# TensorE finds a batch's live chunks with eight nested bodies in place of four loops of two (perceiver block, one core)

## The chip, the cores and the metric

The kernel runs on one core of a Trainium2 chip. The metric is the device time of one execution in microseconds (us), the median of several runs. The kernel is written in Bass: every engine (TensorE or PE, VectorE or DVE, ScalarE or ACT, GpSimd or POOL, SyncE or SP) has a program of its own, and they meet only through semaphores.

## The reference

A block of three layers on x (8 batches, 128 rows, 512 wide): cross-attention to a context, self-attention, and a gated MLP with ternary weights. Only the first matters here:

```python
def xattn(x, context, mask, W_q, W_k, W_v, W_o, b_o):      # x (8,128,512), context (8,2048,384), mask (8,2048)
    q = (x @ W_q).reshape(b, n, 8, 64)
    k = (context @ W_k).reshape(b, j, 8, 64)
    v = (context @ W_v).reshape(b, j, 8, 64)
    sim = einsum('bihd,bjhd->bhij', q, k) / 8
    sim = where(mask[:, None, None, :], sim, max_neg)
    out = einsum('bhij,bjhd->bihd', softmax(sim), v).reshape(b, n, 512)
    return out @ W_o + b_o
x = x + xattn(layernorm(x), ctx, mask, ...)
x = x + self_attention(layernorm(x), ...)
x = x + ffn(layernorm(x), ...)
```

The mask is true only for the last keys of a batch, from 0 to 512 of the 2048, a number drawn for each batch. Keys that are masked out of a batch with any live key have no weight in the softmax.

## The kernel before, in words

The context of a batch is cut into NC = 8 chunks of 256 keys. A chunk with no live key needn't be computed. So the kernel first makes 64 bits, one for each chunk of each batch (a batch without any live key counts all its chunks as live), and each engine loads them into two registers (`live_chunks`, L239). All engines then walk the same list: a loop over the 8 batches (L773 on PE), in it a loop over four groups of two chunks (L778), and in that `live_in_window` (L268). It takes the group's two bits into `left`, shifts the word, and runs its body as often as bits are set: a branch (`If_ne(left, 0)`, L274), two register operations that clear the lowest bit (L275, L276), the body, and in it once more the branch and the body. A group without a live chunk thus jumps over two bodies. At the end of a batch `next_batch` moves the words on by eight bits (L256 to L258).

The body (`chunk`, L677 on PE, L1064 on ScalarE, L1463 on VectorE) does the attention of the current chunk, interleaved with the work for the next live one: `turn_context` (L647, L651) transposes the next chunk's context, `keys` and `values` project it in split precision (three products each, L587). `scores` (L690) for head pairs 0 to 3, `turn` (L705), which transposes the probabilities, and `attend` (L717) are the current chunk's. VectorE's `top` (L1472) takes a head's scores with the mask's bias, writes them to `probs` and the running maximum to `negm`; scores of the next pair wait for it. ScalarE exponentiates (L1069) and then casts the context's high part (L1052). The context of a chunk (cx) is loaded by SyncE.

Behind a batch's last chunk PE does `project_output` of the batch before (L764, from batch 1 on), `turn_output` (L745: the normalised output on_c, which VectorE makes at L1517) and from batch 2 on `turn_norm` (L753). ScalarE and VectorE split the transposed results into high and low parts (onT_hi, onT_lo), VectorE also makes the low part of the next batch's queries (qT_lo). Then each engine walks to the next batch's first live chunk on its own; nothing but the body's semaphores holds one engine to another.

Of the kernel before, what the change touches and what calls it, by code (L numbers as in the profile page):

```python
# [5 lines left out]
ALU = mybir.AluOpType  # L6
# [19 lines left out]
def bass_perceiver_block_kernel(nc, x, ctx_768, mask, xa_wq, xa_wk, xa_wv, xa_wo, xa_bo,  # L26
# [17 lines left out]
    NC = S // CHUNK  # L44
# [11 lines left out]
    with ExitStack() as ctx:  # L56
# [182 lines left out]
        def live_chunks(eng):  # L239

            eng.wait_ge(code_packed, START + 1)
            words = []
            for w in range(CODES // 2):
                low_half = eng.value_load(code[0:1, 2 * w:2 * w + 1], min_val=0, max_val=65535)
                high_half = eng.value_load(code[0:1, 2 * w + 1:2 * w + 2], min_val=0, max_val=65535)
                bits = eng.alloc_register(f"live_chunks{w}")
                eng.reg_mov(bits, high_half)
                eng.reg_alu(bits, bits, 16, ALU.logical_shift_left)
                eng.reg_alu(bits, bits, low_half, ALU.bitwise_or)
                words.append(bits)  # L250
            return words, eng.alloc_register("live_flag")

        def next_batch(eng, words, carry):

            low_word, high_word = words
            eng.reg_alu(carry, high_word, 32 - NC, ALU.logical_shift_left)  # L256
            eng.reg_alu(high_word, high_word, NC, ALU.logical_shift_right)
            eng.reg_alu(low_word, low_word, carry, ALU.bitwise_or)  # L258
# [6 lines left out]

        WINDOW = 2

        def live_in_window(eng, words, left, flag, body):  # L268

            eng.reg_alu(left, words[0], (1 << WINDOW) - 1, ALU.bitwise_and)  # L270
            eng.reg_alu(words[0], words[0], WINDOW, ALU.logical_shift_right)

            def nest(depth):
                with eng.If_ne(left, 0):  # L274
                    eng.reg_alu(flag, left, 1, ALU.subtract)  # L275
                    eng.reg_alu(left, left, flag, ALU.bitwise_and)  # L276
                    body()
                    if depth > 1:
                        nest(depth - 1)

            nest(WINDOW)

        UNITS = 2 * PAIRS

# [289 lines left out]
        def _(pe):  # L574
# [42 lines left out]
            words, flag = live_chunks(pe)  # L617
            left = pe.alloc_register("window_left")
# [122 lines left out]
            def turn_output(b):  # L741

                pe.wait_ge(on_done, START + b + 1)
                for k in range(DK):
                    last = tr(bank[5][:, k * P:(k + 1) * P], on_c[:, k * P:(k + 1) * P], ident[:])  # L745
                last.then_inc(onT_ps, 1)

            def turn_norm(b):

                pe.wait_ge(xn_c_done, START + b + 1)  # L750
                pe.wait_ge(lnT_lo, START + b)
                for k in range(DK):
                    last = tr(bank[6][:, k * P:(k + 1) * P], xn_c[:, k * P:(k + 1) * P], ident[:])  # L753
                last.then_inc(lnT_ps, 1)

            def project_output(b):

                pe.wait_ge(xo_done, START + b)
                n = 0

                for a, c in (("hi", "hi"), ("hi", "lo"), ("lo", "hi")):
                    pe.wait_ge(onT_lo if a == "lo" else onT_hi, START + b + 1)
                    for k in range(DK):
                        last = mm(bank[4][:], part(onT, a)[:, k, :], part(wo, c)[:, k, :], start=(n == 0), stop=(n == 3 * DK - 1))  # L764
                        n += 1
                last.then_inc(xo_ps, 1)
# [6 lines left out]
            with pe.Fori(0, B) as b:  # L773
                def live_chunk():
                    chunk(b, pe.snap(done))
                    pe.reg_add(done, done, 1)

                with pe.Fori(0, NC // WINDOW) as c:  # L778
                    live_in_window(pe, words, left, flag, live_chunk)
                next_batch(pe, words, flag)  # L780
                chunks = pe.snap(done)
                pe.wait_ge(negm_done, START + H * chunks)
                with pe.If(b > 0):
                    project_output(b - 1)
                turn_output(b)
                with pe.If(b > 1):
                    turn_norm(b - 2)
# [222 lines left out]
        def _(act):  # L1010
# [113 lines left out]
            with act.Fori(0, B) as b:  # L1124
                def live_chunk():
                    chunk(b, act.snap(done))
                    act.reg_add(done, done, 1)

                with act.Fori(0, NC // WINDOW) as c:
                    live_in_window(act, words, left, flag, live_chunk)  # L1130
                next_batch(act, words, flag)
                with act.If(b < B - 1):
                    query_high(b + 1, act.snap(done))
                with act.If(b > 0):
                    projected(b - 1)
                output_high(b)
                with act.If(b > 1):
                    norm_high(b - 2)
# [209 lines left out]
        def _(dve):  # L1348
# [207 lines left out]
            with dve.Fori(0, B) as b:  # L1556
                def live_chunk():
                    chunk(b, dve.snap(done))
                    dve.reg_add(done, done, 1)

                with dve.Fori(0, NC // WINDOW) as c:
                    live_in_window(dve, words, left, flag, live_chunk)
                next_batch(dve, words, flag)
                chunks = dve.snap(done)
                with dve.If(b > 1):
                    norm_stats(b - 2)
                normalise(b, chunks)
                with dve.If(b > 1):
                    norm(b - 2)
                with dve.If(b < B - 1):  # L1570
                    query_low(b + 1)
                output_low(b)
                with dve.If(b > 1):
                    norm_low(b - 2)
# [274 lines left out]
```

## Time and profile before

| what | value |
|---|---|
| median of 3 runs | 767.38 us (766.2 to 770.09) |
| profiled execution, its own time | 768.35 us |
| its span, first to last instruction | 765.2 us |
| TensorE's granted clock, mean | 0.945 |
| PE matmul busy | 666.9 us (87% of the span) |
| VectorE busy | 443.9 us (58%) |
| ScalarE busy | 356.4 us (47%) |
| PE in the chain that ended last | 66% |

The span is divided by stage: projections of the queries to about 57 us, the attention over the context with its walk to about 377 us, then the self-attention and the MLP. Rows with PEldq, DVEq or ACTq are the engines' sequencers: branches and register operations, which count as busy for no engine. The instruction queues q8 and q14 in the DMA part bring code.

### The profile page before, as it was taken

The numbers are of one execution on the slowest core, as the hardware profiler recorded it, in microseconds if no ns is written. First come the engines' busy times: TensorE is split into PE (matmuls) and PEld (weight loads), VectorE is DVE, ScalarE is ACT, GpSimd is POOL, SyncE is SP. The second block draws the span as 40 slices with busy tenths as digits, with TensorE's granted clock in tenths as the row PEclk, the third lists the DMA queues.
The fourth block names the chain that finished last, engine by engine and source line by source line (L and its number), as shares of the span: only waits on it lengthen the run. The fifth ranks groups of instructions, "written<-read, shape, count | busy, mean of one in ns | idle before, by whom it ended". The sixth has DMA issues, their size and how long they took to land.

```text
span 765.2 us, 14274 instructions
## 1 busy us (share of the span) xinstructions
PE 666.9 (87%) x4217; PEld 524.4 (69%) x4244; DVE 443.9 (58%) x960; ACT 356.4 (47%) x846; POOL 109.0 (14%) x143
## 2 busy tenths in 40 slices
PE   2898698979889779979879889999999899889996
PEld 1677587868778668868758667777777778534553
DVE  6823444554545453545567756666666544699974
ACT  2234233434434333434410146666666443568984
POOL 2681000010100110010100012222221100012121
PEclk9999798979989897989989989999999999999999
DMA  8000000000000000004169834445553343000111
GB/s 314 26 23 24 24 2 21 22 22 22 2 21 22 22 2 21 22 22 140 69 205 301 290 110 166 166 166 165 166 165 139 136 140 124 1 1 15 27 27 41
DMA packets 40067, 64.91 MB, mean 85 GB/s; under 512 B 4056, under 2 KB 20440, under 8 KB 40032
## 3 DMA queue, kind: packets, MB, share of 16 engines
q1 hardware_dynamic: 40032, 64.45, 25.1%
q8 instruction: 21, 0.34, 0.2%
q14 instruction: 14, 0.11, 0.0%
HBM read 53.95 MB, written 10.49 MB: 84 GB/s over the span
## 4 chain that ended last, share of the span: by engine, by line
PE 66%; DVE 13%; issue 9%; DMA 4%; ACT 3%; DVEq 3%; POOL 1%; SPq 1%; ACTq 0%; POOLq 0%
PE bank L587 35%; PE bank L717 6%; PE bank L949 5%; PE bank L705 3%; DMA absw<-in_L_ffn_w_down_dram 3%; PE bank L690 3%; PE bank L957 2%; PE bank L864 2%; DVE asum L1607 2%; DVE tern L1657 2%; PE bank L606 2%; DVE xn_a L1374 1%; PE bank L841 1%; PE bank L899 1%; PE bank L852 1%
## 5 line engine op out<-in xcount | busy, mean ns | idle before, releaser
L1069 ACT ACTIVATE probs<-probs,negm 128x256 f32<-128x256 f32 x104 | 52.1, 501 | 87.1 <-DVE negm L1472 86.5
L1472 DVE CUSTOM_DVE_ANT_0 probs<-bank,bias,negm_old 128x256 f32<-128x256 f32 x104 | 46.0, 480 | 42.4 <-PE bank L690 42.4
L949 PE MATMUL bank<-w_T,xqT 128*128 128x512 bf16 x248 | 57.3, 379 | 5.3 <-ACT xqT L1252 2.0
L717 PEld LDWEIGHTS bank<-v_sb,pT 128*128 128x128 f32 x416 | 52.3, 191 | 5.5
L484 POOL TENSOR_TENSOR rstd<-var_eps,neg_half 128x1 f32 (+1 forms) x16 | 10.0, 625 | 320.9 <-DVE var_eps L1535 249.8
L1363 DVE TENSOR_TENSOR kT_lo<-bank,kT_hi 128x512 fp32r<-128x512 f32 x28 | 19.4, 692 | 62.0 <-ACT kT_hi L1058 62.0
L717 PE MATMUL bank<-v_sb,pT 128*128 128x64 f32 x416 | 54.7, 274 | 0.0
L1062 ACT COPY v_sb<-bank 128x512 f32<-128x512 f32 x28 | 15.1, 590 | 76.5 <-PE bank L717 73.5
L690 PE MATMUL bank<-kT_hi,qT_hi 64*128 64x256 f32 x104 | 23.0, 433 | 29.6 <-issue 27.2
L949 PEld LDWEIGHTS bank<-w_T,xqT 128*128 128x128 bf16 x256 | 24.1, 98 | 34.9 <-issue 2.9
L587 PE MATMUL bank<-cxT_hi,wk_hi 128*128 128x256 f32 x168 | 38.4, 342 | 4.6 <-ACT cxT_hi L1052 4.6
L690 PEld LDWEIGHTS bank<-kT_hi,qT_hi 64*128 64x128 f32 x104 | 11.9, 212 | 39.0 <-issue 28.7
L530 POOL TENSOR_TENSOR p_even<-p_even,rsum 128x512 f32<-128x512 f32 x16 | 18.1, 1131 | 118.6 <-DVE rsum L1636 118.6
L705 PE MATMUL bank<-ident,probs 128*128 128x128 f32 x208 | 33.9, 289 | 0.0
L1607 DVE TENSOR_REDUCE asum<-absw 128x3072 f32 x8 | 26.8, 3351 | 10.6 <-DMA absw<-in_L_ffn_w_down_dram 10.6
L587 PEld LDWEIGHTS bank<-cxT_hi,wk_hi 128*128 128x128 f32 x168 | 27.3, 217 | 8.2 <-ACT cxT_hi L1052 7.4
L1626 DVE COPY kT<-bank 128x512 f32<-128x512 f32 x16 | 11.1, 692 | 37.0 <-PE bank L587 37.0
L587 PE MATMUL bank<-cxT_lo,wk_hi 128*128 128x256 f32 x168 | 31.8, 301 | 0.5 <-DVE cxT_lo L1363 0.5
L587 PE MATMUL bank<-cxT_hi,wk_lo 128*128 128x256 f32 x168 | 32.2, 305 | 0.0
L1173 ACT ACTIVATE p_odd<-bank,nmax 128x128 f32<-128x128 f32 x64 | 22.7, 371 | 15.7 <-DVE nmax L1632 15.7
L1187 ACT ACTIVATE tern_raw<-tern_raw,wscale 128x1024 f32<-128x1024 f32 x24 | 26.9, 1163 | 4.0 <-DVE tern_raw L1651 4.0
L587 PEld LDWEIGHTS bank<-cxT_lo,wk_hi 128*128 128x128 f32 x168 | 27.0, 209 | 0.8 <-DVE cxT_lo L1363 0.7
(236 smaller groups left out, 1692.1 us busy)
## 6 DMA issues: line engine op xcount, KB each, us to landing
tern_dram<-tern SPq DMA_DIRECT2D x8, 768.0 KB, 5.4
tstage<-tern_dram SPq DMA_DIRECT2D x8, 768.0 KB, 4.4
cx<-in_ctx_dram SPq DMA_DIRECT2D x14, 384.0 KB, 3.0
absw<-in_L_ffn_w_gate_dram SPq DMA_DIRECT2D x8, 512.0 KB, 3.8
absw<-in_L_ffn_w_up_dram SPq DMA_DIRECT2D x8, 512.0 KB, 5.4
absw<-in_L_ffn_w_down_dram SPq DMA_DIRECT2D x8, 512.0 KB, 6.8
tern_raw<-in_L_ffn_w_gate_dram SPq DMA_DIRECT2D x8, 512.0 KB, 6.4
tern_raw<-in_L_ffn_w_up_dram SPq DMA_DIRECT2D x8, 512.0 KB, 7.1
```

What stands on the lines that cost most here:

```text
L530: nc.gpsimd.tensor_tensor(p, p, r, ALU.mult).then_inc(pn_done, 1)
L587: last = mm(to, left(k, a), right(k, b), start=(n == 0), stop=(n == 3 * nk - 1))
L690: last = mm(bank[3 + j][:, 0:CHUNK], part(qT, a)[o:o + DH, g, :], part(kT, c)[o:o + DH, g, :], start=(a == c), stop=(a == "lo"))
L705: last = tr(bank[5 + g % 2][:, at:at + P], probs[:, 2 * g + j, t * P:(t + 1) * P], ident[:])
L717: last = mm(bank[7][:, h * DH:(h + 1) * DH], pT[:, g % 2, at:at + P], v_sb[:, t, h * DH:(h + 1) * DH], start=(t == 0), stop=(t == CT - 1))
L949: last = mm(bank[3 + 2 * which + c % 2][:], xqT[:, u, k * P:(k + 1) * P], w_T[:, which, k, c * 512:c * 512 + 512], start=(k == 0), stop=(k ...
L1069: fn(probs[:, h, :], probs[:, h, :], ACT.Exp, bias=negm[:, h:h + 1], scale=-1.0, accum_out=csum[:, h:h + 1]).then_inc(p_done, 1)
L1173: last = fn(p2[u % 2][j][:, g * P:(g + 1) * P], bank[2 + j][:, g * P:(g + 1) * P], ACT.Exp, bias=nmax2[:, j, g:g + 1], scale=SCALE, accum_ ...
L1187: made = fn(piece, piece, ACT.Copy, bias=ROUND, scale=wscale[:, w:w + 1])
L1363: return tt(to, of, f32(hi), ALU.subtract)
L1472: nc.vector.tensor_tensor_reduce(probs[:, h, :], bank[3 + h % 2][:, 0:CHUNK], bias[:], -SCALE, negm_old[:, h:h + 1], ALU.add, ALU.min, neg ...
L1607: red(asum[:, bass.ds(g, 1), :].rearrange("p a w -> p (a w)"), absw[u][:], AX_X, ALU.add, apply_absolute_value=True).then_inc(absw_done, 1)
```

## The change

`live_in_window` gets its number of bits as an argument. PE calls it once for a batch with all NC = 8 bits, so that its code has eight nested bodies, and has no loop over groups any more. ScalarE and VectorE keep their loops of four groups of two. SyncE has its own walk, chunk by chunk, and keeps it.

```diff
-        def live_in_window(eng, words, left, flag, body):
-
-            eng.reg_alu(left, words[0], (1 << WINDOW) - 1, ALU.bitwise_and)
-            eng.reg_alu(words[0], words[0], WINDOW, ALU.logical_shift_right)
+        def live_in_window(eng, words, left, flag, body, size=WINDOW):
+
+            eng.reg_alu(left, words[0], (1 << size) - 1, ALU.bitwise_and)
+            eng.reg_alu(words[0], words[0], size, ALU.logical_shift_right)
...
-            nest(WINDOW)
+            nest(size)
...
-                with pe.Fori(0, NC // WINDOW) as c:
-                    live_in_window(pe, words, left, flag, live_chunk)
+                live_in_window(pe, words, left, flag, live_chunk, NC)
                 next_batch(pe, words, flag)
```

PE's program at the start of the batch loop, before. L773 is the loop over batches, L778 the loop over groups, L270 to L276 the walk, L690 the first scores of body 0:

```order
L773 UNCONDITIONAL_BRANCH
L778 UNCONDITIONAL_BRANCH
L270 REGISTER_ALU
L271 REGISTER_ALU
L274 COMPARE_AND_BRANCH
L275 REGISTER_ALU
L276 REGISTER_ALU
```

and the same place after the change:

```order
L773 UNCONDITIONAL_BRANCH
L270 REGISTER_ALU
L271 REGISTER_ALU
L274 COMPARE_AND_BRANCH
L275 REGISTER_ALU
L276 REGISTER_ALU
```

The walk enters body 0 directly. The end of the last body and the batch's tail on PE, before (L717 is the last `attend`, L764 `project_output`):

```order
L717 MATMUL bank<-v_sb,pT 128x64 x4
L776 REGISTER_ALU
L274 UNCONDITIONAL_BRANCH
L778 REGISTER_ALU
L778 COMPARE_AND_BRANCH
L256 ISA
L258 REGISTER_ALU
```

and after, at the end of body 7 (the lines below the change are one lower):

```order
L717 MATMUL bank<-v_sb,pT 128x64 x4
L776 REGISTER_ALU
L274 UNCONDITIONAL_BRANCH
L256 ISA
L258 REGISTER_ALU
```

The loop's back edge over groups is gone. Between the two places PE's program had two bodies and now has eight; the matmuls of its whole program go from 2114 to 2810 as they are written (a body has 116). The programs of the other engines are the same instruction by instruction.

## Rows read from the trace of the kernel before

**Rows 1.** The page, section 2: TensorE's granted clock in 40 slices, tenths.
```profile
PEclk9999798979989897989989989999999999999999
```

**Rows 2.** PE sequencer: xcount, ns min/median/max, first to last start in us.
```profile
L776 PEldq ALU_OP  x13: 32/32/32, 80.6 to 371.3; - x13
...
L778 PEldq COMPARE_BRANCH  x32: 67/208/242, 61.0 to 371.5; - x32
...
L274 PEldq COMPARE_BRANCH  x4: 75/210/215, 86.2 to 88.8; - x4
```

**Rows 3.** Timeline, starts of batches 1 and 3: start, us, work [idle before <-releaser].
```profile
85.14 1.11 PE L745 MATMUL bank<-ident,on_c 128*128 128x128 f32 x4 [2.42 <-DVE on_c L1517]
...
89.56 0.58 PE L690 MATMUL bank<-kT_hi,qT_hi 64*128 64x256 f32 x2 [3.31 <-issue]
...
90.15 0.42 PE L690 MATMUL bank<-kT_hi,qT_lo 64*128 64x256 f32 x2
...
92.22 0.58 PE L690 MATMUL bank<-kT_hi,qT_hi 64*128 64x256 f32 x2 [0.18 <-DVE negm L1472]
...
160.04 0.66 PE L745 MATMUL bank<-ident,on_c 128*128 128x128 f32 x4 [0.66 <-DVE on_c L1517]
```

**Rows 4.** Chain in order of time: start, us, what; starts of batches 1, 3.
```profile
88.17 0.06 DVEq L274
...
90.58 0.05 DVEq L274
...
91.27 0.11 DVE probs L1472
...
165.71 0.05 DVEq L274
...
166.38 0.11 DVE probs L1472
```

**Rows 5.** Batch 0's start: timeline, then the branch L274 on PE and on VectorE.
```profile
63.98 0.58 PE L690 MATMUL bank<-kT_hi,qT_hi 64*128 64x256 f32 x2 [2.99 <-issue]
...
65.16 0.48 DVE L1472 CUSTOM_DVE_ANT_0 probs<-bank,bias,negm_old 128x256 f32<-128x256 f32 x1 [6.92 <-PE bank L690]
...
L274 PEldq COMPARE_BRANCH  x1: 3535/3535/3535, 57.3 to 57.3; - x1
...
L274 DVEq COMPARE_BRANCH  x1: 50/50/50, 62.7 to 62.7; - x1
```

**Rows 6.** DMA queues: packets, MB, share; 36-94, 100-380 (q1 is all), 400-702 us.
```profile
q8 instruction: 6, 0.10, 0.8%
...
q1 hardware_dynamic: 4502, 8.14, 9.0%
...
q8 instruction: 15, 0.25, 0.3%
```

**Rows 7.** Stretches: length, busy us (xcount) by engine, PEclk, DMA share, GB/s.
```profile
138.30:156.50 18.20, 17.33 (x133) 15.46 (x134) 9.20 (x29) 8.41 (x25) 0.00 (x0) 1.00 0.08 23
89.55:110.80 21.25, 20.89 (x133) 18.70 (x134) 8.51 (x28) 7.45 (x23) 0.00 (x0) 0.80 0.06 19
400.00:702.00 302.00, 277.37 (x1777) 209.30 (x1795) 198.62 (x340) 157.72 (x399) 42.40 (x53) 0.98 0.42 143
84.40:98.10 13.70, 9.30 (x44) 7.99 (x44) 4.75 (x14) 4.10 (x12) 0.00 (x0) 0.50 0.09 29
```

**Rows 8.** Ends of batches 0, 1: branches of PE, then timeline of 1.
```profile
L274 PEldq COMPARE_BRANCH  x1: 429/429/429, 80.7 to 80.7; - x1
...
L274 PEldq COMPARE_BRANCH  x1: 207/207/207, 108.8 to 108.8; - x1
...
L783 PEldq COMPARE_BRANCH  x1: 82/82/82, 109.7 to 109.7; - x1
...
110.61 1.18 PE L764 MATMUL bank<-wo_hi,onT_hi 128*128 128x512 f32 x4
...
113.46 0.60 PE L745 MATMUL bank<-ident,on_c 128*128 128x128 f32 x4
```

## The prediction

> **What bounds the kernel now.** I read the page first: in the first half of the span, where the attention over the context runs, PEclk goes between 7 and 9 tenths [rows 1], so the clock falls there again and again. The change touches only how PE finds its live chunks, so the question is who is late at a batch's start and at its end. The chunk body runs 13 times (L776 x13) [rows 2] in 8 batches: so three batches have one live chunk and five two, always the last ones of the batch's eight, so PE, VectorE and ScalarE each pass three empty groups of two before the one that works. For PE that is 4 groups x 8 batches, the 32 of L778 [rows 2].
>
> The price of an empty group is in the register rows of PE's sequencer [rows 2]: two ALU operations, a taken COMPARE_BRANCH of 207 ns at L274, an ALU and another taken branch of 208 ns at L778; four L274 branches lie between 86.2 and 88.8 us, so a group costs PE (88.8 - 86.2) / 3 = 0.87 us, three of them 2.6 us. The timeline of batch 1's start shows this as PE idle for 3.31 us "<-issue" [rows 3]. That looks like 8 x 2.6 = 21 us to gain. But the chain of work over the same stretch [rows 4] doesn't run through PE there: it runs through VectorE's own walk (four branches DVEq L274, the first at 88.17 and the last at 90.58, so 0.80 us a group) to the first row maximum at 91.27. PE's first scores are out at 90.15 + 0.42 = 90.57, or 0.7 us before VectorE can read them. What PE does after the transposes waits for VectorE again (scores 1 at 92.22, "<-DVE negm" [rows 3]). The chain passes through the same DVEq rows at the start of batch 3: the last branch at 165.71, the maximum at 166.38 [rows 4]. So at seven of the eight starts VectorE, whose walk is not changed, ends last.
>
> **The change part by part.**
> Three empty groups leave PE at each start. Batches 1 to 7: PE's scores 0 and its transposes of the context come up to 2.6 us earlier, and then PE waits for the same negm at the same time. Gain 0: VectorE's walk covers it. If that cover were gone too, the 3.31 us of idle PE would be worth at most 2.6 us a batch, 18 us.
> Batch 0 is different. VectorE's last L274 branch is at 62.7 [rows 5], and in batch 1 it needs 91.27 - 90.58 = 0.7 us from there to the first maximum [rows 4], so it is ready at 63.4; it starts at 65.16, released by PE [rows 5], whose scores begin at 63.98 after 2.99 us of issue. Now they can begin where the queue of values ends, at 61.0, and be out at 62.0. VectorE then bounds: the gain is 65.16 - 63.4 = **1.8 us**, once (ends: 0, if something else is late, and 2.99, PE's whole gap).
> The first scores and the transposes also let cx be loaded earlier; its consumer is a whole chunk of 18 us away [rows 7], so 0. SP, POOL, VectorE and ScalarE have the same instructions as before.
>
> Seven copies of code come in. At the end of a batch's last live chunk the branch at L274 now jumps over six or seven bodies, not over one or none. What a jump to code that isn't loaded costs PE is in the trace once: the first L274 branch of the kernel, over two bodies that have not been run, took 3535 ns at 57.3 us, against 207 for the others [rows 5]. It cost nothing there, since PE still had matmuls queued to 61.0. Six packets of PE's instruction queue (q8, 16 KB each) came in between 36 and 94 us, and none from 100 to 380 us, where q1 is the only queue listed [rows 6], while the loop ran seven more times. So PE keeps the whole loop of before. How much is that? Between 400 and 702 us 15 packets came while PE ran 1777 matmuls and 1795 weight loads [rows 6, 7]: about 240 of these to a packet, some 255 with register work. One body is 266 matmuls and loads (133 and 134 in 18.2 us) [rows 7] and some 25 others, so 1.15 packets; the loop of before is two bodies and the batch's tail, 2.6 packets; that of after is eight and a tail, **9.5 packets** from top to end. Of these only the top, bodies 0 and 1 and the tail are ever run, about 3 or 4 packets with the next one fetched ahead each time, 6 or 7. The trace shows that 2.6 packets in a row stay; it does not show whether two pieces 7 packets apart do.
>
> The Trainium skill (Runtime: NRT & Kernel Launch, Instruction fetch mechanics) says that an engine holds its current window of two pages and that a taken branch out of it stalls for a fetch; the loop of before is 2.6 packets long and fetched nothing in seven passes, so for PE the trace does not agree with the two pages. The same section gives TensorE room for 2048 instructions, that is 8 pages; by that capacity the loop of before fits and the one of after, 9.5 packets, does not.
>
> Price of one such miss at a batch's end. The branch takes 3.53 instead of 0.21 us, 3.3 more. In batch 1 it is issued at 108.80, the next one (L783) at 109.7, so project_output could be issued at about 110.1; it begins at 110.61, without a gap behind the chunk [rows 8]. With 3.3 us more it begins at 113.4, 2.8 us late, and since turn_output follows it at once (113.46, no idle) all of that is lost. In batches 2 to 7 the sequencer is as far ahead, but turn_output waits anyway: in batch 3, PE is idle for 0.66 us before 160.04 [rows 3], which leaves 2.0 to 2.1. VectorE has work of its own queued there, which may cover a part; between nothing and 2.0 I take 1.7, near the upper end, since the whole start of the next batch hangs on what turn_output gives. In batch 0 there is no projection; the miss from 80.7 [rows 8] runs to 84.3, the register work of 1.2 us after it (L274 to the first matmul, as in batch 1) to 85.5, and turn_output stands at 85.14 behind on_c [rows 3], so 0.3 is left. One miss is certain, in batch 0, where that code is first reached: **+0.3 us**.
>
> Sum for the profiled execution, 768.35 us: -1.8 + 0.3 = 766.9. The median of the three runs is 767.38, 1.0 lower, so **766.0 us** if the code stays loaded. Below 0.5% (3.8 us) a measurement of this kernel can't tell from no change.
>
> **The rivals.**
> Recurring fetch (slower). Where the code at the tail and that at the top push each other out, the branch at the end of each batch costs 3.3 us again: 0.3 + 2.8 + 6 x 1.7 = 13.3, less 1.8: +11.5, so 779 us. If only batches with two live chunks do it (they fetch one packet further), 0.3 + 5 x 1.7 - 1.8: +7, 774 us. For it: 9.5 packets, more than any loop of the trace; and six packets came between 36 and 94 us although the loop's code is only 2.6 long, so some may have come twice. Against: none came for the next seven passes. This decides from a loss of 3.8 us on, that is from three batches with a miss. The back edge can miss too; PE has 2.6 + 0.7 = 3.3 us of slack there, just the price, so this alone costs nothing. Chance 0.32. The Trainium skill's 2048 instructions, in the section named above, speak for this rival.
> Two misses a batch (slower). If body 0 also has to be fetched again in its middle, PE stalls with full queues behind it: 1.3 to 3.3 us in seven batches, +9 to +23 on top, 788 to 802 us. For: a straight run into the next packet has always been fetched ahead in the trace, so against it more than for. Chance 0.06.
> Clock (faster). PE is granted 0.50 of its clock (1.2 GHz) from 84.4 to 98.1 us, behind the idle stretch of batch 1's start, and 1.00 (2.4 GHz) from 138.3 to 156.5 [rows 7]; a first chunk takes 21.25 us (batch 1, clock 0.80), a second one 18.2 at 1.00. Scores that come 2.6 us earlier split the idle stretch in another way. If that kept the clock up in three of eight starts, 3 x 2.5 = 7.5 us, plus the 1.8: 758 us. Against: PE's busy time is the same and the gap of 3.3 us is only moved behind the transposes, which could as well take 2 to 3 us. Chance 0.10 for the faster side.
> That the change doesn't do what it says gets nothing: the order of the instructions shows PE's bodies eight deep and the loop of groups gone.
>
> **How the numbers follow.** Code stays loaded, 766.0: 0.52 (764 to 769 with the ends of batch 0's gain and one more miss). Recurring fetch 0.32 and two misses 0.06, 0.38 slower by over 0.5%. Faster by over 0.5%: 0.10. The range takes in the forecast less 3.5 us of the clock's case, and the recurring fetch with its bound of 2.0 us a batch (0.3 + 2.8 + 6 x 2.0 - 1.8 = +13.3, 781) and 2 us for the clock: **762.5 to 783**. Left out are two misses and most of the faster case, 0.14.
>
> **What would show it.** Right: L1472's first maximum of batch 0 near 63.4 us; PE's gap before the scores of batches 1 to 7 down from 3.3 to about 0.7 us, with a new one of about 3 us "<-DVE negm" behind the transposes; chain through DVEq L274 as before; L274 branches of PE at 207 ns but for one of 3.5 us near 79 us; q8 packets silent from 100 to 380 us. Wrong: L274 branches of 3.5 us in most batches with q8 packets beside them (recurring fetch); stalls inside a chunk (two misses); fewer stretches at 0.50 (clock); or batches 1 to 7 each shorter by more than 1 us, which would mean that VectorE is not the last at their start.

## The result and the profile after

The changed kernel takes 775.15 us (median of 6 runs, 771.14 to 780.39) against 766.79 us for the kernel before (6 runs): ratio 1.011, 95% interval 1.0076 to 1.0144. It is slower by 8.4 us. The profiled execution of the changed kernel took 775.04 us with a span of 772.9 us, 7.7 us more than that of before. Lines of the changed kernel are one lower behind L778 (VectorE's maximum is L1471, ScalarE's exponential L1068, the branch at the tail L782).

The page of the changed kernel, its sections 1 to 4, where [rows 1, 6] have their like:

```profile
PE 668.5 (86%) x4244; PEld 523.8 (68%) x4244; DVE 443.4 (57%) x960; ACT 356.6 (46%) x846; POOL 108.9 (14%) x143
...
PEclk9999798988989987998979999999999999999999
...
q8 instruction: 25, 0.41, 0.2%
...
PE 69%; issue 10%; DVE 10%; POOL 4%; ACT 3%; DVEq 3%; ACTq 0%; POOLq 0%
```

and the code queue's line of the kernel before:

```profile
q8 instruction: 21, 0.34, 0.2%
```

PE does the same work. The code queue q8 brought 25 packets against 21. I compared the two traces by VectorE's first maximum of each batch (L1472, L1471 in the changed kernel), in us:

| | before | changed | later by |
|---|---|---|---|
| batch 0 | 65.16 | 63.41 | -1.75 |
| batch 1 | 91.27 | 93.65 | +2.38 |
| batch 2 | 118.89 | 120.70 | +1.81 |
| batch 3 | 166.38 | 173.66 | +7.28 |
| batch 4 | 213.99 | 221.54 | +7.55 |
| batch 5 | 260.09 | 269.34 | +9.25 |
| batch 6 | 289.97 | 300.13 | +10.16 |
| batch 7 | 337.24 | 347.89 | +10.65 |
| batch 7, second chunk | 355.84 | 368.32 | +12.48 |

Four things happened: a gain at batch 0, a step of 4.1 us at its end, one of 5.5 us at the end of batch 2, and a drift of 5.2 us from batch 3 to the end. Behind the attention 4.8 of the 12.5 us came back.

**Batch 0's start** went as forecast. Timeline of the changed kernel, against [rows 5]:

```profile
60.90 0.38 PE L690 MATMUL bank<-kT_hi,qT_hi 64*128 64x256 f32 x2
...
63.41 0.48 DVE L1471 CUSTOM_DVE_ANT_0 probs<-bank,bias,negm_old 128x256 f32<-128x256 f32 x1 [5.19 <-issue]
```

PE's scores begin at 60.90 right behind the queue of values, and VectorE, ready at 63.4, is now the last.

**The two steps** are long branches. The branches of PE's sequencer in the changed kernel (xcount, ns min/median/max, first to last start), by stretch: about 80 us, 84 us, 156 us, and all from 165 to 390 us:

```profile
L274 PEldq COMPARE_BRANCH  x1: 3872/3872/3872, 80.2 to 80.2; - x1
...
L782 PEldq COMPARE_BRANCH  x1: 2892/2892/2892, 84.5 to 84.5; - x1
...
L274 PEldq COMPARE_BRANCH  x1: 3854/3854/3854, 156.1 to 156.1; - x1
...
L274 PEldq COMPARE_BRANCH  x13: 66/66/208, 191.4 to 383.9; - x13
```

and what PE waited for behind them, timeline:

```profile
87.52 1.11 PE L745 MATMUL bank<-ident,on_c 128*128 128x128 f32 x4 [5.36 <-issue]
...
160.69 0.79 PE L764 MATMUL bank<-wo_hi,onT_hi 128*128 128x512 f32 x1 [2.64 <-issue]
163.15 1.44 PE L764 MATMUL bank<-wo_hi,onT_hi 128*128 128x512 f32 x3 [1.67 <-issue]
164.39 1.91 PE L764 MATMUL bank<-wo_lo,onT_hi 128*128 128x512 f32 x4
166.09 1.72 PE L764 MATMUL bank<-wo_hi,onT_lo 128*128 128x512 f32 x4
167.65 0.60 PE L745 MATMUL bank<-ident,on_c 128*128 128x128 f32 x4
```

At the end of batch 0 the jump over seven bodies took 3.87 us; the tail's code lies across two packets, and the next branch in it (L782) took 2.89 us, because the second packet wasn't there either. turn_output came at 87.52 in place of 85.14 us [rows 3]. At the end of batch 2, the first batch with two live chunks, there is one more of 3.85 us, and inside project_output a second wait of 1.67 us. PE's clock also fell to half at about 160.5 us, after the idle stretch, so that most of the twelve matmuls of project_output, which are 512 wide, ran at 1.2 GHz (length, busy us of PE, PEld, DVE, ACT, POOL with xcount, PEclk, DMA share, GB/s):

```profile
160.40:167.30 6.90, 4.94 (x11) 3.77 (x12) 2.00 (x5) 0.00 (x0) 0.56 (x1) 0.52 0.01 2
```

No branch was long after that: the longest of the other 13 took 208 ns.

The code queue shows the order at batch 2. One packet came between 150 and 156 us, that is before the long branch at 156.1, while PE was still in the second chunk; two more came between 156 and 166 us; from 166 to 380 us there was none:

```profile
q8 instruction: 1, 0.02, 1.0%
...
q8 instruction: 2, 0.03, 1.6%
```

**The drift** has no fetch in it. It comes in batches 3 (+0.3), 4 (+1.7), 5 (+0.9), 6 (+0.5) and 7 (+1.8), inside the first chunk. The first chunks of the changed kernel all take about the same (20.4 to 20.5 us in batches 3, 4, 6 and 7); those of the kernel before took 20.2, 18.8, 19.9 and 18.6 us, so most of the drift is that two short ones are gone. Maxima of batch 4's two chunks, changed kernel:

```profile
221.54 0.48 DVE L1471 CUSTOM_DVE_ANT_0 probs<-bank,bias,negm_old 128x256 f32<-128x256 f32 x1 [2.87 <-issue]
...
241.99 0.48 DVE L1471 CUSTOM_DVE_ANT_0 probs<-bank,bias,negm_old 128x256 f32<-128x256 f32 x1
```

and before:

```profile
213.99 0.48 DVE L1472 CUSTOM_DVE_ANT_0 probs<-bank,bias,negm_old 128x256 f32<-128x256 f32 x1 [2.87 <-PE bank L690]
...
232.75 0.48 DVE L1472 CUSTOM_DVE_ANT_0 probs<-bank,bias,negm_old 128x256 f32<-128x256 f32 x1
```

20.45 us in place of 18.76. The stretches at half clock there (columns as above), of the changed kernel:

```profile
221.90:228.70 6.80, 6.04 (x30) 5.52 (x30) 2.36 (x10) 3.51 (x11) 0.00 (x0) 0.51 0.01 5
```

and of the kernel before:

```profile
210.70:217.50 6.80, 4.79 (x24) 4.08 (x25) 2.70 (x10) 1.83 (x6) 0.00 (x0) 0.50 0.17 46
```

Both are 6.8 us at 0.50 (1.2 GHz). Before, it began with PE idle ahead of the scores, 3.3 us ahead of the maximum, and PE had 4.8 us of work in it. In the changed kernel it began 0.4 us behind the maximum and PE had 6.0 us of work in it, which at 2.4 GHz takes about half as long (four matmuls 512 wide: 1.91 us here, 1.08 there, in the rows of L587 below). By that the changed kernel loses 3.0 us there and the other 2.4, so 0.6 of the 1.7 us is told by the amount of work in the stretch. The rest would be in which work it was (ahead of the maximum, or behind it); I didn't separate that. The kernels below that drift too have 20.3 to 20.4 us in this chunk with another stretch, 10.2 us long from about 3 us ahead of the maximum, so neither the length of the stretch nor the work in it gives the time by itself. stall_like, batch 4:

```profile
218.00:228.20 10.20, 8.16 (x40) 7.25 (x40) 3.24 (x11) 3.51 (x11) 0.00 (x0) 0.50 0.12 39
```

**What came back.** Behind the attention PE waits for the mean of the MLP's weights. Before:

```profile
439.98 0.59 PE L815 MATMUL bank<-asum,ones 128*128 128x3 f32 x2 [2.57 <-DVE asum L1614]
440.43 2.05 PE L587 MATMUL bank<-ln_T_hi,wqk_even_hi 128*128 128x512 f32 x4
442.28 1.91 PE L587 MATMUL bank<-ln_T_hi,wqk_even_lo 128*128 128x512 f32 x4
443.99 1.91 PE L587 MATMUL bank<-ln_T_lo,wqk_even_hi 128*128 128x512 f32 x4
```

and changed:

```profile
450.26 0.39 PE L814 MATMUL bank<-asum,ones 128*128 128x3 f32 x2
450.51 1.17 PE L587 MATMUL bank<-ln_T_hi,wqk_even_hi 128*128 128x512 f32 x4
451.52 1.08 PE L587 MATMUL bank<-ln_T_hi,wqk_even_lo 128*128 128x512 f32 x4
452.44 1.08 PE L587 MATMUL bank<-ln_T_lo,wqk_even_hi 128*128 128x512 f32 x4
```

Before, PE had been waiting 2.57 us there and its clock had fallen, so the next twelve matmuls took until 445.9; in the changed kernel the weights were in time, nothing was idle and they took 3.0 us. That is 2.5 us of the 4.8; the mean itself is only 10.3 us later instead of 12.5.

### The profile page after: what moved, and what is told of

Read it like the earlier page. It is cut to its first block, busy times and chain, and to the rows that moved or that the text cites. A ratio compares the mean times of both kernels' runs of the same rounds, so it can differ in the third digit from the quotient of the medians.

```text
span 772.9 us, 14167 instructions
## 1 busy us (share of the span) xinstructions
PE 668.5 (86%) x4244; PEld 523.8 (68%) x4244; DVE 443.4 (57%) x960; ACT 356.6 (46%) x846; POOL 108.9 (14%) x143
## 4 chain that ended last, share of the span: by engine, by line
PE 69%; issue 10%; DVE 10%; POOL 4%; ACT 3%; DVEq 3%; ACTq 0%; POOLq 0%
PE bank L587 39%; PE bank L717 6%; PE bank L948 5%; PE bank L705 3%; PE bank L690 2%; PE bank L956 2%; PE bank L863 2%; DVE tern L1656 2%; POOL x_all L513 1%; PE bank L840 1%; PE bank L898 1%; PE bank L764 1%; PE bank L851 1%; ACT cxT_hi L1051 1%; DVE h_f L1761 1%
## 5 line engine op out<-in xcount | busy, mean ns | idle before, releaser
L1068 ACT ACTIVATE probs<-probs,negm 128x256 f32<-128x256 f32 x104 | 52.1, 501 | 85.7 <-DVE negm L1471 85.1
L1471 DVE CUSTOM_DVE_ANT_0 probs<-bank,bias,negm_old 128x256 f32<-128x256 f32 x104 | 46.0, 480 | 40.9 <-issue 27.2
L717 PEld LDWEIGHTS bank<-v_sb,pT 128*128 128x128 f32 x416 | 52.3, 191 | 5.5
L717 PE MATMUL bank<-v_sb,pT 128*128 128x64 f32 x416 | 54.7, 274 | 0.0
L690 PE MATMUL bank<-kT_hi,qT_hi 64*128 64x256 f32 x104 | 22.0, 420 | 33.8 <-DVE negm L1471 28.7
L587 PE MATMUL bank<-cxT_hi,wk_hi 128*128 128x256 f32 x168 | 39.7, 352 | 5.2 <-ACT cxT_hi L1051 5.2
L690 PEld LDWEIGHTS bank<-kT_hi,qT_hi 64*128 64x128 f32 x104 | 10.9, 205 | 43.6 <-DVE negm L1471 32.1
L587 PEld LDWEIGHTS bank<-cxT_hi,wk_hi 128*128 128x128 f32 x168 | 28.5, 226 | 8.7 <-ACT cxT_hi L1051 8.0
L587 PE MATMUL bank<-cxT_lo,wk_hi 128*128 128x256 f32 x168 | 33.9, 316 | 0.5 <-DVE cxT_lo L1362 0.5
L587 PE MATMUL bank<-cxT_hi,wk_lo 128*128 128x256 f32 x168 | 33.3, 313 | 0.0
L587 PEld LDWEIGHTS bank<-cxT_lo,wk_hi 128*128 128x128 f32 x168 | 28.7, 223 | 0.8 <-DVE cxT_lo L1362 0.7
L587 PEld LDWEIGHTS bank<-cxT_hi,wk_lo 128*128 128x128 f32 x168 | 28.4, 223 | 0.0
```

The source lines that it names most:

```text
L587: last = mm(to, left(k, a), right(k, b), start=(n == 0), stop=(n == 3 * nk - 1))
L690: last = mm(bank[3 + j][:, 0:CHUNK], part(qT, a)[o:o + DH, g, :], part(kT, c)[o:o + DH, g, :], start=(a == c), stop=(a == "lo"))
L717: last = mm(bank[7][:, h * DH:(h + 1) * DH], pT[:, g % 2, at:at + P], v_sb[:, t, h * DH:(h + 1) * DH], start=(t == 0), stop=(t == CT - 1))
L1068: fn(probs[:, h, :], probs[:, h, :], ACT.Exp, bias=negm[:, h:h + 1], scale=-1.0, accum_out=csum[:, h:h + 1]).then_inc(p_done, 1)
L1471: nc.vector.tensor_tensor_reduce(probs[:, h, :], bank[3 + h % 2][:, 0:CHUNK], bias[:], -SCALE, negm_old[:, h:h + 1], ALU.add, ALU.min, neg ...
```

## The experiments

Ratios are to the kernel before, timed beside each run on the same chip: its medians there were 764.46 us (pe_four, pe8_late, skip_all, pe8_skip), 763.82 us (stall_like, skip_dve_act, pe_one, dve_late) and 764.56 us (pe8_both, skip_again).

**pe_four: half as much code.** PE walks two groups of four bodies.

```diff
-                live_in_window(pe, words, left, flag, live_chunk, NC)
+                with pe.Fori(0, NC // 4) as c:
+                    live_in_window(pe, words, left, flag, live_chunk, 4)
```

> PE walks two groups of four nested bodies; the loop is about 4.9 packets of code from top to end, so it would fit where 2.6 does. Theory A (neighbour): PE's instruction buffer fetches the next packet ahead without regard to what is already in it, and that pushes out the tail, which was fetched out of order; misses come once each time a longer straight run is made for the first time: L274 branches of 3.5 us or more at 57 us (hidden), at the end of batch 0 and at the end of batch 2, the first with two live chunks, then none. Attention end 3 to 10 us later than before (377 us), time 768 to 773 us. Rival B (capacity): the misses of the eight-body kernel come because 9.5 packets do not fit; then there is only the hidden one at 57 us here, and the time is 765 to 768 us.

Measured: 769.94 us, ratio 1.006 (1.0035 to 1.0085). PE's branches L274 at 58.8, 80.5 and 153.9 us, and all later ones:

```profile
L274 PEldq COMPARE_BRANCH  x1: 3508/3508/3508, 58.8 to 58.8; - x1
...
L274 PEldq COMPARE_BRANCH  x1: 3402/3402/3402, 80.5 to 80.5; - x1
...
L274 PEldq COMPARE_BRANCH  x1: 3672/3672/3672, 153.9 to 153.9; - x1
...
L274 PEldq COMPARE_BRANCH  x17: 75/207/213, 186.5 to 378.6; - x17
```

Three long branches, at the three places that theory A names, and none at the ends of the five batches that follow, though the loop's code is half as long. So the misses don't come from 9.5 packets being too many; rival B falls. The maxima are 0.7 us early at batch 2, 2.6 us late at batch 3, and 7.2 us late at the end: a drift of 4.6 us here too.

At batch 0's end this kernel has the single miss that the prediction had priced: the tail's next branch (L783 here) is short in all batches, and turn_output stands at 85.00 us behind on_c, as before the change (85.14 [rows 3]). The single miss cost nothing that can be seen.

```profile
L783 PEldq COMPARE_BRANCH  x8: 77/77/249, 84.6 to 379.5; - x8
...
85.00 0.65 PE L745 MATMUL bank<-ident,on_c 128*128 128x128 f32 x4 [2.48 <-DVE on_c L1517]
```

**pe8_both: the longest straight run first.** The changed kernel, in which every batch has two live chunks: in three batches one chunk is computed whose keys are all masked, so its time has 3 chunks more and isn't compared.

```diff
+                eng.reg_alu(bits, bits, 0x40404040, ALU.bitwise_or)
```

> The changed kernel with the bit of chunk 6 set in every batch on every engine: the three batches with one live chunk now compute one more, whose keys are all masked, so 3 chunks of 18 us are added and only the branches are to be compared. Theory A (a straight run that gets farther than any before it fetches the next packet over the tail's): batch 0 already runs bodies 0 and 1, so the farthest run is made before the tail is first fetched; long branches only at the end of batch 0 (one or two), none at the end of batch 1, 2 or later. Rival I (the tail's packets fall out of the buffer for another reason, with time or after some passes): one more at the end of batch 2 or nearby.

Measured: 821.53 us in one run. Branches of PE (L275 is the walk's here, L783 the tail's), at 98 us, at 102 us, and all of the walk from 110 us on:

```profile
L275 PEldq COMPARE_BRANCH  x1: 3822/3822/3822, 98.1 to 98.1; - x1
...
L783 PEldq COMPARE_BRANCH  x1: 3177/3177/3177, 102.4 to 102.4; - x1
...
L275 PEldq COMPARE_BRANCH  x20: 66/70/217, 129.4 to 431.1; - x20
```

Two long branches at batch 0's end, where the tail is first reached, and none at batch 2 or elsewhere. Rival I falls. Together with pe_four and the packet that came ahead of the long branch of batch 2: the tail's packet is lost when the straight run gets one packet farther than before for the first time, as if the packet fetched ahead took its place. That it takes that place is an inference from these orders, not a thing that a row shows, and pe8_both is one run.

**stall_like: the stalls without the code.** The kernel before with empty loops on PE where the long branches were.

```diff
                 with pe.Fori(0, NC // WINDOW) as c:
                     live_in_window(pe, words, left, flag, live_chunk)
+                with pe.If(b < 3):
+                    with pe.If(b < 1):
+                        with pe.Fori(0, 17) as idle:
+                            pass
+                    with pe.If(b > 1):
+                        with pe.Fori(0, 10) as idle:
+                            pass
```

> The kernel before, with its two bodies, and empty loops on PE in the places of the changed kernel's long branches: 17 passes (some 6.2 us; the two branches there took 3.7 + 2.8 us too long) behind batch 0's chunk, 10 passes (3.6 us) behind batch 2's, two short branches in the others. Theory A2 (three late fetches are the whole loss): the maxima move as in the changed kernel, by +4 us at batch 1, +7 to +8 at batch 3 and the rest, up to +12, in batches 4 to 7 without any stall there; time 772 to 777 us. Rival G (the eight bodies cost something else too, in every batch): +4 and +4 only, nothing in batches 4 to 7, time 768 to 771 us.

Measured: 777.17 us, ratio 1.016 (1.0095 to 1.0226). The maxima are later by 3.76 (batch 1), 3.84 (2), 7.50 (3), 7.40 (4), 8.91 (5), 9.71 (6), 10.13 (7) and 11.89 us at the last chunk. With two bodies of code and no packet of q8 from 94 us to the end of the attention, the whole pattern is there, the drift too (4.4 us). So stalls at those two places are enough for the loss, and rival G falls: nothing is left that the eight bodies would have to cost in a batch where their code is loaded. The match is not exact: the loops idle PE 1 us longer at batch 0, batch 0's gain is mostly missing, and the loss by the medians is 13.3 us, more than the changed kernel's 8.4, with intervals that overlap. The timeline of batch 0's end:

```profile
88.90 1.11 PE L745 MATMUL bank<-ident,on_c 128*128 128x128 f32 x4 [6.41 <-issue]
```

**pe8_late: PE's scores at their old time.** The changed kernel with seven empty passes (2.6 us) ahead of PE's walk.

```diff
+                with pe.Fori(0, 7) as idle:
+                    pass
                 live_in_window(pe, words, left, flag, live_chunk, NC)
```

> The changed kernel with a loop of seven empty passes ahead of PE's walk at every start of a batch, so that PE's first scores come at the old time again (2.6 us later). Theory C (clock): in the changed kernel part of the loss, some 5 of the 12.5 us by the end of the attention, comes in batches 3 to 7 without any fetch, because the earlier scores move the stretch at 0.50 from the idle time into the dense part of the chunk; then the first chunks of batches 4 and 7 (22.8 us maximum to maximum in the changed kernel's trace, against 18.8 before) lose less and the time falls to 769 to 773 us. Rival D (the loss is all in the three misses): the time stays at 775 or rises by the 1.8 us of batch 0.

Measured: 776.24 us, ratio 1.0143 (1.008 to 1.0206). The maxima are +9.37 at batch 4, +11.01 at batch 5 and +14.19 at the last chunk: the drift from batch 3 on is 5.0 us, as in the changed kernel. Theory C falls in its form: the earlier scores don't cause the drift. What the kernels with a drift share (the changed one, pe_four, stall_like, pe8_late) is that everything from batch 3 on is 2.6 to 9.2 us later, and that the first chunks of batches 4 and 7 take 20.3 to 20.5 us with PE's half-clock stretch elsewhere: in the changed kernel 6.8 us long from 0.4 us behind the maximum, in the other three 10.2 us long from about 3 us ahead of it. What decides between these wasn't tried, and the cause of the drift stays open. Read the other way, the run says that PE's 2.6 us at a start are free when the code is there: only batch 0's gain (1.6 us at its maximum) is lost.

**skip_all and skip_again: the walk of all three engines.** Two new operations and a branch ahead of the groups; the last two chunks have code of their own.

```diff
+        def skip_dead(eng, words, rest, left, flag, body):
+
+            eng.reg_alu(rest, words[0], (1 << (NC - WINDOW)) - 1, ALU.bitwise_and)
+            eng.reg_alu(words[0], words[0], NC - WINDOW, ALU.logical_shift_right)
+            with eng.If_ne(rest, 0):
+                with eng.Fori(0, NC // WINDOW - 1) as c:
+                    live_in_window(eng, [rest], left, flag, body)
+            live_in_window(eng, words, left, flag, body)
...
-                with pe.Fori(0, NC // WINDOW) as c:
-                    live_in_window(pe, words, left, flag, live_chunk)
+                skip_dead(pe, words, rest, left, flag, live_chunk)
```

and the same for ScalarE and VectorE.

> All three engines test the first six bits of a batch with one branch and jump over a loop of three groups where none is set; the last two chunks have code of their own (four bodies on each engine). Theory E (VectorE ends last at a batch's start): its walk loses 2.4 us and gains about 0.4, so each of batches 1 to 7 begins 2.0 us earlier and batch 0 1.8 us: 14 to 16 us less, 751 to 754 us, plus up to 3 us for a miss or two. Rival F (something else, ScalarE or the loads, stands right behind VectorE): less than 8 us gained, 760 or more.

> The kernel of skip_all once more, for its interval: 745 to 749 us, ratio to before 0.970 to 0.980.

Measured: 746.8 us, ratio 0.9727 (0.9652 to 0.9803); again, with more executions, 742.99 us, ratio 0.9726 (0.9696 to 0.9756). It beats both kernels, by 21 us that of before. Batch 1's start in the second of them (L700 is the scores', L1482 the maximum's line):

```profile
84.61 0.58 PE L700 MATMUL bank<-kT_hi,qT_hi 64*128 64x256 f32 x2 [1.04 <-issue]
...
86.29 0.48 DVE L1482 CUSTOM_DVE_ANT_0 probs<-bank,bias,negm_old 128x256 f32<-128x256 f32 x1 [1.29 <-PE bank L700]
```

The maximum is 5.0 us earlier than the 91.27 of [rows 4], 2.5 of it from batch 0, 2.5 at this start. More was gained than the 14 to 16 us that were expected of the walk. The attention of this kernel (columns as above):

```profile
57.00:355.00 298.00, 270.87 (x1865) 235.61 (x1864) 149.24 (x454) 125.73 (x353) 16.37 (x19) 0.94 0.09 30
```

against that of the kernel before:

```profile
57.00:377.00 320.00, 278.51 (x1867) 242.61 (x1866) 152.28 (x456) 126.26 (x354) 16.17 (x21) 0.90 0.09 28
```

PE has 7.6 us less of busy time for the same matmuls, at a mean clock of 0.94 in place of 0.90. So a part of the gain is clock; how much of it wasn't separated, and that the shorter idle stretches are what keeps it up is likely but not shown.

**pe8_skip: the change with that skip on the others.** ScalarE and VectorE as in skip_all, PE as in the changed kernel.

> PE as in the changed kernel (eight nested bodies), ScalarE and VectorE with the one-branch skip. By theory E the changed kernel's 775 us fall by 2.0 us for each of seven starts, to 759 to 763 us, still behind skip_all by the misses (7 to 10 us). By rival F 768 us or more.

Measured: 754.01 us, ratio 0.9853 (0.9803 to 0.9903). By the ratios that is 1.3% or 10 us behind skip_all, by the medians 7 us, and the three long branches are there (3.8, 2.7 and 3.4 us). It is better than expected by 5 us; I didn't look for the cause.

**skip_dve_act: PE alone keeps the slow walk.**

> ScalarE and VectorE with the one-branch skip, PE with its four groups as before. Theory E (VectorE ends last at a start, PE 0.7 us ahead of it): once VectorE is 2 us earlier PE's walk is the last, so only 0.7 us a start is left, some 5 us of the 17.7 that the skip on all engines gained: 758 to 761 us. Rival H (PE's walk never matters): the whole 17 us, 747 us.

Measured: 757.87 us, ratio 0.9917 (0.9889 to 0.9945). Batch 1's start (L699 is the scores'):

```profile
89.19 0.58 PE L699 MATMUL bank<-kT_hi,qT_hi 64*128 64x256 f32 x2 [3.40 <-issue]
...
90.36 0.48 DVE L1482 CUSTOM_DVE_ANT_0 probs<-bank,bias,negm_old 128x256 f32<-128x256 f32 x1 [3.15 <-PE bank L699]
```

VectorE now waits for PE's scores. The gain is 6 of the 18 us by which skip_all's median is lower, near the 5 that 0.7 us a start would give; rival H falls.

**pe_one: a longer walk on PE.** One body, eight groups; the edit is against the changed kernel.

```diff
-                live_in_window(pe, words, left, flag, live_chunk, NC)
+                with pe.Fori(0, NC) as c:
+                    live_in_window(pe, words, left, flag, live_chunk, 1)
```

> PE walks eight groups of one body: six or seven empty ones before the first live chunk in place of three, so 3.0 to 3.5 more at 0.87 us each. With 0.7 us of slack at a start PE becomes the last by 2 to 2.5 us a start: +16 to +20 us, and 0 to 0.5 us between two live chunks; 780 to 786 us. If PE's walk had far more slack than 0.7 us: under 772. No long branch except perhaps the first, since the code is 1.5 packets.

Measured: 783.2 us, ratio 1.0251 (1.0205 to 1.0298), +19 us. Batch 1's start:

```profile
98.16 0.73 PE L690 MATMUL bank<-kT_hi,qT_hi 64*128 64x256 f32 x2 [6.61 <-issue]
...
99.32 0.48 DVE L1472 CUSTOM_DVE_ANT_0 probs<-bank,bias,negm_old 128x256 f32<-128x256 f32 x1 [6.07 <-PE bank L690]
```

PE idles 6.61 us, and VectorE waits 6.07 us for it.

**dve_late: a longer walk on VectorE.** The kernel before with three empty passes ahead of VectorE's. They were taken for 1.1 us; the trace shows 0.8.

```diff
+                with dve.Fori(0, 3) as idle:
+                    pass
                 with dve.Fori(0, NC // WINDOW) as c:
```

> The kernel before with a loop of three empty passes (1.1 us) ahead of VectorE's walk. By theory E each of batches 1 to 7 starts 1.1 us later, batch 0 not at all (VectorE waits 1.8 us for PE there): +7 to +8 us, 771 to 773 us. If VectorE's walk is not last: +0 to 2 us.

Measured: 770.88 us, ratio 1.0083 (1.0055 to 1.0111), +6.4 us by the ratio. At batch 1 the maximum is at 91.89 and PE's scores were out at 90.43:

```profile
89.42 0.58 PE L690 MATMUL bank<-kT_hi,qT_hi 64*128 64x256 f32 x2 [3.32 <-issue]
...
90.01 0.42 PE L690 MATMUL bank<-kT_hi,qT_lo 64*128 64x256 f32 x2
...
91.89 0.48 DVE L1472 CUSTOM_DVE_ANT_0 probs<-bank,bias,negm_old 128x256 f32<-128x256 f32 x1 [4.08 <-issue]
```

VectorE's walk is on the path and PE's isn't. The loop itself (L1561) lies between 87.79 and 88.55 us in the chain, 0.76 us, where L1563 is the loop over groups:

```profile
87.79 0.04 DVEq L1561
...
88.55 0.04 DVEq L1563
```

From batch 3 on each start comes 0.8 us later, counted from the second chunk's maximum (28.2 us in place of 27.4). So what was added to VectorE's walk shows in full. The passes were shorter than assumed, and the time is just below the 771 to 773 us expected.

## Why the prediction was wrong

The forecast was 766.0 us, no measurable change; it came out 8.4 us slower. That this lies inside the range of 762.5 to 783 is luck: the range reached so far for a recurring fetch, which didn't happen.

- Who ends last at a batch's start: right. VectorE's walk sets it and PE has 0.7 us of slack. dve_late, pe_one and skip_dve_act bear it out from three sides. So of the 21 us that PE's idle rows promise the change could have only batch 0's 1.8, and got 1.75.
- The failed step is "one miss is certain, in batch 0: +0.3 us", with its reason that packets either stay or push each other out at every pass. Three branches were long, once each: two at batch 0's end and one at batch 2's. The choice between "code stays loaded" and "recurring fetch" left out the case between: packets move while the loop is new to the buffer and stay when it isn't. The hint was in the rows: six packets in [rows 6] for a loop of 2.6, so some may have been fetched twice. I used it for a recurring fetch, but not to ask when the second copies were fetched.
- The price of what came was too low. For a single miss in batch 0 the prediction's 0.3 us was about right: pe_four has it and loses nothing there. In the changed kernel the miss was double, because the tail spans two packets, and moved the next maximum by 4.1 us. In batch 2 it was 5.5 us, not 1.7: 2.6 us of idle, 1.7 more for the packet behind, and half the clock for what followed.
- The drift of 5.2 us in batches 4 to 7 was in no step. The clock stood among the rivals as a gain from the earlier scores; no such gain came, and pe8_late shows that the earlier scores don't cause the drift either. Its cause stays open.
- That a delay in the attention isn't passed on in full (12.5 us there, 7.7 at the end) was not considered either; the next stage had a wait of 2.57 us and a clock that fell in it.
- The rival of a recurring fetch in five batches, 774 us, is near the measured time for the wrong reason: one late fetch, not five, lies in those batches.

The Trainium skill (Runtime: NRT & Kernel Launch, Instruction fetch mechanics) says that a taken branch out of the current two-page window stalls. For PE the jump over six or seven bodies (7 to 8 packets, at the prediction's 1.15 a body) stalled at its first use and once more, and took at most 208 ns in the passes after (in pe_four, with four bodies, 213 ns), so by the trace more than two pages stay. Its 2048 instructions don't bound a loop's length from top to end either: 9.5 packets with a hole in them ran without a fetch from batch 3 on.

## What to carry to other kernels

Where engines walk the same list on their own, the idle rows of one engine are no gain until the chain of waits runs through that engine; here shortening the walk on all three gave 21 us and on PE alone nothing but batch 0's 1.8. Code that is laid out eight times but run twice cost a few late fetches of 3 to 4 us each here. A single one can hide behind a wait (pe_four, batch 0); where it doesn't, it can cost more than its length, since the clock falls behind it (5.5 us at batch 2 for waits of 4.3). Skipping what is empty with one branch, with the live code next to the tail, got the short walk with only the long branch at 57 us that the kernel before had too.

## What the runs showed that was not expected

- With four bodies (4.9 packets) as with eight, the jump to PE's tail was long twice and not again afterwards, the second time when a packet had just been fetched ahead. That this packet took the place of one that was still wanted is the inference that fits. The long branches took 3.4 to 3.9 us, and the one into the packet right behind 2.7 to 3.2 us.
- A delay of some us early in a stage changed later batches by up to 1.8 us each, and with it TensorE's half-clock stretch. In batch 4 it is 6.8 us long with 4.8 us of PE's work in it before, 6.8 us with 6.0 in the changed kernel, and 10.2 us with 8.2 in stall_like. That this makes up the whole drift wasn't shown.
- An empty pass of a loop costs PE's sequencer 0.37 us (17 passes begin between 81.6 and 87.6 us in stall_like) and VectorE's about 0.26 (three in 0.76 us with the loop's entry, in dve_late).
